# A conv, FFN and mixture-of-experts kernel: GpSimd scales the coming input first in each body and sends the routing's list entries in shares of one, two and one group

## The reference, cut to what matters

```python
x: (128, 32, 512)                                   # 4096 rows of 512
# four modulated 1-D convolutions over 32 channels, kernel 3; per layer:
s = style @ mw.T + mb
weight = SCALE * w * s[:, None, :, None]            # s scales the input channels
weight = weight * rsqrt(sum(weight * weight) + EPS)
out = conv(x, weight) + b                           # same, upsample+blur, same, blur+downsample
# feed-forward over the 4096 rows h that come out:
scores = sigmoid(h @ gate_w.T) + bias               # 16 experts
topk_w, topk_idx = top_k(scores, 4);  topk_w /= sum(topk_w)
out = sum over the 4 chosen experts of topk_w * (silu(h @ Wg[e].T) * (h @ Wu[e].T)) @ Wd[e].T
out = out + silu(h @ Sg.T) * (h @ Su.T) @ Sd.T      # shared expert
return x + out
```

## Time and profile before

| | |
|---|---|
| median of 3 executions | 1262.66 us (1261.3 to 1268.32) |
| the profiled execution, its own time | 1263.14 us |
| its span in the profile | 1261.3 us |
| TensorE busy, share of the span | 1146.1 us, 91% |
| VectorE, ScalarE, GpSimd busy | 805.2, 495.3, 576.1 us |
| mean granted TensorE clock | 0.963 of full speed |
| convolution stage with its tail | from 0 to about 576 us |
| expert stage | from about 576 us to the end |

### The profile page before, as it was taken

How to read it: one execution, slowest core, us unless ns; L and a number is a source line. 1 busy time by engine, 2 the same in 40 slices (tenths; PEclk the granted TensorE clock), 3 DMA queues, 4 the chain that set the end, 5 groups by cost and what they waited for, 6 DMA issues and landing times. The chain is left out here.

```text
span 1261.3 us, 24476 instructions
## 1 busy us (share of the span) xinstructions
PE 1146.1 (91%) x7149; PEld 1008.8 (80%) x7150; DVE 805.2 (64%) x1947; ACT 495.3 (39%) x1149; POOL 576.1 (46%) x667
## 2 busy tenths in 40 slices
PE   4899898999989898863999999999999999999995
PEld 2787676777767677642999999999998899999995
DVE  8777676767767675754665565655657565555653
ACT  4656455545555454421332232323233332222321
POOL 2100423233241405164565656666665565666663
PEclk9999999998989998965999999999999999999998
DMA  6755555554545454314667667666766777666664
GB/s 225 175 152 149 120 133 134 133 133 116 143 102 145 112 136 106 85 43 115 149 120 154 120 150 120 133 138 115 159 112 154 190 126 157 110 108 114 111 113 75
DMA packets 140376, 163.58 MB, mean 130 GB/s; under 512 B 31456, under 2 KB 97088, under 8 KB 138816
## 3 DMA queue, kind: packets, MB, share of 16 engines
q0 software_dynamic: 35696, 74.34, 33.0%
q1 hardware_dynamic: 104320, 88.63, 26.0%
q10 hardware_dynamic: 336, 0.32, 0.1%
HBM read 74.58 MB, written 55.18 MB: 103 GB/s over the span
## 5 line engine op out<-in xcount | busy, mean ns | idle before, releaser
L1262 PE MATMUL bank<-xt_hi,wup_hi 128*128 128x256 f32 x1104 | 278.3, 285 | 1.9 <-issue 1.9
L1262 PE MATMUL bank<-xt_hi,wup_lo 128*128 128x256 f32 x1104 | 278.0, 284 | 0.0
L461 POOL DMA_INDIRECT out_rows<-yb,sid x140 | 225.5, 1611 | 90.0 <-DVE yb L1045 66.0
L409 POOL DMA_INDIRECT lists<-entry,place x128 | 128.8, 1006 | 196.4 <-DVE place L859 153.6
L1262 PEld LDWEIGHTS bank<-xt_hi,wup_hi 128*128 128x128 f32 x1104 | 212.6, 193 | 6.2 <-issue 3.7
L1262 PEld LDWEIGHTS bank<-xt_hi,wup_lo 128*128 128x128 f32 x1104 | 213.2, 193 | 2.4
L544 ACT ACTIVATE t<-bank,cB,cA 128x256 f32<-128x256 f32 (+1 forms) x384 | 172.0, 534 | 98.8 <-PE bank L221 96.3
L448 POOL DMA_INDIRECT xg<-h_rows,gid x140 | 141.8, 1013 | 120.7 <-PE bank L1240 77.1
L1266 PE MATMUL bank<-xt_lo,wup_hi 128*128 128x256 f32 x1104 | 178.1, 284 | 0.0
L1045 DVE TENSOR_SCALAR yb<-bank,all_lists 128x512 f32<-128x512 f32 x138 | 99.9, 748 | 87.0 <-DMA out_rows<-yb,sid 55.0
L1266 PEld LDWEIGHTS bank<-xt_lo,wup_hi 128*128 128x128 f32 x1104 | 152.7, 193 | 0.0
(11 more groups left out here) (204 smaller groups left out, 2164.5 us busy)
## 6 DMA issues: line engine op xcount, KB each, us to landing
x<-x1p SPq DMA_DIRECT2D x64, 384.0 KB
wraw<-in_Wup SPq DMA_DIRECT2D x11, 1024.0 KB, 7.7
xraw<-in_xq SPq DMA_DIRECT2D x32, 260.0 KB, 2.8
xbase<-in_x SPq DMA_DIRECT2D x32, 256.0 KB, 2.8
h_rows<-hrow SPq DMA_DIRECT2D x128, 64.0 KB, 2.2
out_rows<-orow SPq DMA_DIRECT2D x32, 256.0 KB, 2.1
x<-x1p SPq DMA_DIRECT2D x64, 127.0 KB
wdraw<-in_Wdn SPq DMA_DIRECT2D x11, 512.0 KB, 9.8
```

What stands on the lines that cost most here:

```text
L409: pool.indirect_dma_start(out=lists, out_offset=bass.IndirectOffsetOnAxis(ap=place[:, home, r, k:k + 1], axis=0), in_=entry[:, home, r, k, ...
L461: pool.indirect_dma_start(out=out, out_offset=bass.IndirectOffsetOnAxis(ap=sid[:, u:u + 1], axis=0), in_=yb[:, u, :], in_offset=None, comp ...
L1262: pe.matmul(dst, lhs[a], rhs[0], start=k == 0 and a == 0, stop=False)
```

## The change

In the loop, GpSimd scales one group at the start of each of the four steps, and only then does it wait for places (first step) and send entries: one group in the first step, two in the second, one in the third, none in the fourth. The loop is one turn shorter, and the last loop round's entries are written out behind it with the last two groups' scaling. Groups 8 and 9 are scaled ahead of the loop. The waits for `x2_ready`, `x3_ready` and `h_ready` ahead of entries are gone. The seventh round gets a home of its own (3), so `mark` doesn't wait there.

```diff
-        place = sb("place", [P, 3, R, TOPK], I32)
-        entry = sb("entry", [P, 3, R, TOPK, 2])
+        place = sb("place", [P, 4, R, TOPK], I32)
+        entry = sb("entry", [P, 4, R, TOPK, 2])
...
-            for g in range(2, 2 * R):
+            for g in range(2, 2 * R + 2):
                 scaled(g, g % 2, g // 2)
 
-            with pool.Fori(0, ROUNDS - 1) as it:
-                coming = lambda r: (it * R + (2 * R + r), r % 2, it * (R // 2) + (2 * R + r) // 2)
+            shares = ((0,), (1, 2), (3,), ())
+            with pool.Fori(0, ROUNDS - 2) as it:
                 for r in range(R):
+                    scaled(it * R + (2 * R + 2 + r), r % 2, it * (R // 2) + (R + 1 + r // 2))
                     if r == 0:
-                        scaled(*coming(0))
-                        scaled(*coming(1))
                         pool.wait_ge(S["place_ready"], it + 1)
-                    else:
-                        pool.wait_ge(S["x2_ready" if r == 2 else "x3_ready"], it * (4 * R) + 4 * (R + 3 + r // 2) + 4)
-                    scatter(2, r, "scattered")
-                    if r == 1 or r == 2:
-                        scaled(*coming(r + 1))
-            assert (ROUNDS - 1) * R + 2 * R == G
+                    for n in shares[r]:
+                        scatter(2, n, "scattered")
+            assert (ROUNDS - 2) * R + 2 * R + 2 == G - 2
+            for r in range(R):
+                if r < 2:
+                    scaled(G - 2 + r, r % 2, G // 2 - 1)
+                if r == 0:
+                    pool.wait_ge(S["place_ready"], ROUNDS - 1)
+                for n in shares[r]:
+                    scatter(2, n, "scattered")
             pool.wait_ge(S["place_ready"], ROUNDS)
-            scatter(2, 0, "scattered")
+            scatter(3, 0, "scattered")
             for r in range(R):
                 if r:
-                    pool.wait_ge(*((S["x3_ready"], (LAST + 1 + r) * 4 + 4) if LAST + 1 + r < G else (S["h_ready"], G)))
-                    scatter(2, r, "scattered")
+                    scatter(3, r, "scattered")
                 pool.wait_ge(S["place_ready"], ROUNDS + r + 1)
                 scatter(r % 2, 0, f"scattered{r % 2}")
...
-                        places(number, 2 if many == R else (number - ROUNDS - 1) % 2, many)
+                        places(number, (number - ROUNDS - 1) % 2 if many < R else 3 if early else 2, many)
...
-                            mark(2, ("scattered", 16 * TOPK * R * (ROUNDS - 1) + 16), R)
+                            mark(3, None, R)
```

## The result

The changed kernel takes 1230.55 us (median of 4, 1226.41 to 1231.64) against 1262.57 for the kernel before (1261.3 to 1268.32): ratio 0.9732, 95% interval 0.9694 to 0.9769. That is faster, by 32.0 us between the medians; the two profiled executions, 1230.12 and 1263.14, differ by 33.0. Forecast were 1228 us and 34.9 us less.

The account below looks back on a forecast made before the run. The prediction took TensorE to bound the kernel, stalled six times in the convolution stage by GpSimd's late scaling. Terms of -38.1 and +3.2 gave -34.9 us, from the median 1262.66 to 1228 us; range 1220 to 1236.

Parts of the forecast that it names:

- What bounds the kernel, and what the change removes: Convolution stage, bodies u = 3: GpSimd scales behind eight indirect DMAs, `x_hi` 6.27 us late; scaling first gains 38.1 us.
- the low clock: Bodies u = 3: TensorE's granted clock of 0.84 or 0.92 belongs to the stall and goes with it.
- the prediction's check from the other side: Gain in the stalled bodies worked out again as six times the lateness of 6.27 us: 37.6 us.
- The moved entries cost nothing: Loop: GpSimd's idle time, some 13 us a body, hides the moved entries; nothing queued behind them comes late; 0 us.
- The two deadlines: Entries must end before the next scaling is wanted (8.4 and 9 us spare) and before `mark` rewrites home 2 (9.9 spare).
- Collisions with VectorE: Bodies u = 2: the scaling now meets VectorE's short steps, costing 0.54 us in each of six bodies, 3.2 us.
- the prediction's bounds: Most gained 42.5 us (1220), including 0.54 given back in each of five u = 0 bodies (2.7); least 29.3 us (1233.4).
- The tail and the expert stage shift as they are: Bodies 29 to 34 and the expert stage keep their order and length and only start earlier; 0 us.
- Entries slowing VectorE: Rival, chance 0.05: twelve entries a round hold up busy VectorE by 0.3 us each; 21.6 us come back, 1249.
- Another cause behind the stall: Rival, chance 0.03: with `x_hi` ready, ScalarE or TensorE waits as long for something else; no change, 1263 us.
- Starved entries: Rival, chance 0.04: busy VectorE keeps GpSimd from writing indirect DMAs, shares grow and `mark` waits; 1305 or about 1289 us.
- The limit worked out for an entry: An indirect DMA may take up to 2.38 us before `mark` waits; each 0.1 us more costs 6 us.

Follow-up runs that it names:

- experiment 5: The changed kernel without the entries of the loop's six rounds: 1228.88 us, one execution; body 29 starts at 462.33 instead of 461.86.
- experiment 2: The changed kernel with all sixteen entries of a round sent at once, behind the first scaling: 1236.63 us, ratio 0.979 to the kernel before.
- experiment 4: The changed kernel with every entry of the loop written twice, the second time to a scratch tensor: 1243.65 us, ratio 0.9842 to the kernel before.
- experiment 3: The changed kernel with one group's entries in each of the four steps: 1253.98 us, ratio 0.9932 to the kernel before.
- experiment 1: The kernel before with one scaling moved, behind four entries instead of eight: 1230.67 us, ratio 0.975.

## Why the prediction was right

*What bounds the kernel, and what the change removes.* Right, and shown from three sides: with eight, four and no indirect DMAs ahead of the scaling, `x_hi` is 6.27, 1.2 and 0 us late, and the six bodies sum to 125.73, 94.51 and 88.37. The term was 38.1 and measured 37.4; the missing 0.7 is in bodies 12 to 24, at 14.81 to 14.84 instead of 14.60. With the scaling and no entries they are 14.6 (experiment 5), and with entries and no scaling too (experiment 2), so neither costs it alone. What does stays open: experiment 4 has both in these bodies, at 14.6. The prediction took the low clock as part of the stall, and that held: in the six bodies TensorE's idle time fell from 26.65 to 2.2 us and its busy time from 99.08 to 86.2. So 24.5 us of the 37.4 were waiting, and 12.9 were matmuls that ran longer while the granted clock was 0.84 or 0.92. That the two add up to just six times the lateness of 6.27 us, the prediction's check from the other side, no run explains.

*The moved entries cost nothing.* Right for these shares. The two deadlines on which it rested are real: passing that of the next scaling cost 1.3 us a round for 1.8 of lateness (experiment 2), passing that of `mark` 4.8 for 3.4 on average (experiment 3).

*Collisions with VectorE.* Right in kind, a little small: 4.0 us in bodies u = 2 instead of 3.2. By the lock rule that the prediction quoted from the Trainium skill (SBUF — State Buffer, "SBUF: two separate sides") the term was 5.2, so the measurement lies between the two. What I hadn't seen is that bodies u = 0 would lose theirs: from body 13 on the load is issued 2.7 to 3.2 us into the body instead of 2.3 to 2.4, so the scaling comes a little later against VectorE's chain, at 228.15. In bodies 13, 21 and 25 it is GpSimd that waits (1.48 us there), and in body 17 nothing collides. That gave 1.7 back. What delays the load isn't shown; without entries (experiment 5) it is issued at 2.0. The 1.7 lies inside the 2.7 that the prediction's bounds allowed for it, but its sum had nothing there.

*The tail and the expert stage shift as they are.* They took 0.7 and 1.3 us more. In all the kernels profiled the expert stage took 680.9 to 683.3 us with the same work, so 1.3 is not to be told from chance.

*Sum.* 37.4 - 4.0 + 1.7 + 0.4 - 0.4 - 0.7 - 1.3 = 33.1 against 33.0 measured and 34.9 forecast. That it comes so near owes a little to luck: the terms that the forecast had at nothing are -2.4 and +2.1, and nearly cancel.

*The rivals.* Entries slowing VectorE: refuted by experiment 5, nothing gained without them, and by experiment 2, where bodies full of them last 14.6. Another cause behind the stall: refuted by experiment 1. Starved entries: GpSimd's indirect DMAs beside busy VectorE took 0.97 us with single ones up to 1.5, so the 3.1 us that the same section of the skill reports for such a DMA isn't seen here. The limit worked out for an entry, 2.38 us, was about right: with 2.56 (experiment 4) `mark` waited in two turns of five. That limit assumed a landing of 3.1 us; entries landed in 2.1, which puts the limit by the same sum at 2.47.

## What to carry to other kernels

On an engine that works in order, give first place to the short step that another engine waits for next, and fit long bookkeeping behind it by deadlines: each share must end before the next such step, and before whoever rewrites its buffer. In this loop waiting past a deadline cost on average 0.7 to 1.4 times the wait, and far before it nothing was gained, so by the medians moving half of the work was as good as moving all. Then look at where the freed step falls: here GpSimd's 1 us of arithmetic, started as soon as its data came, hit VectorE's chain in most bodies, and waiting on purpose for VectorE's idle time was worth another 12 us, 9.8 of them read from the loop's own bodies.

## What the runs showed of the hardware

- A wait's price depends on which wait it is, and not on its length alone. `x_hi` late by 1.2, 1.8 and 6.27 us lengthened the loop's bodies by 1.15, 1.5 and 6.2, at granted clocks of 1.00, 1.00 and 0.84 to 0.92. `mark`'s waits, 3.4 us on average and 3.86 at most, lengthened theirs by 4.0 on average, and the next body by 0.8, at clock 0.88 to 0.95, so part of that was spent at the lower level.
- A VectorE step can be held up by a GpSimd TENSOR_TENSOR that by the profile hasn't begun, where an indirect DMA ran in front of that on GpSimd. The step of experiment 4 shown above began at 234.64, the scaling at 235.05, and the step ended at 236.67, 1.34 us longer than its 0.69. Plainer still is a 64x4 CAST of the same run, 0.17 us by itself, that began 0.42 us before the scaling's recorded start at 466.04 and ended with it, at 467.1. Starts on GpSimd are rough in the profile, so whether the scaling really began later isn't shown. VectorE's timeline, then GpSimd's:

```profile
465.62 1.51 DVE L942 CAST x_hi<-t3f 64x4 fp32r<-64x4 f32 x1
```
```profile
466.04 1.06 POOL L392 TENSOR_TENSOR xraw<-xraw,s 128x520 f32<-128x520 f32 x1
```

- With no entry in front, such a collision lengthened a 64x4 step by 0.86 us in the kernel before (1.03 instead of 0.17) and by 0.90 in body 11 of the changed one.
